# Splitting the F2 and F3 products of a convolution into odd and even nodes, with their differences on GpSimd

## The chip, the cores and the metric

One NeuronCore of a Trainium2 chip. The metric is the device time of one execution in microseconds; the kernel before takes 300.03 us (median of 3 runs, 299.94 to 300.22).

## The reference, cut to what matters

32 graphs of 256 nodes with 128 features each, all in fp32. One layer:

```python
xc = transpose(x)                                        # (32, 128 features, 256 nodes)
h = relu(bn1(conv1d(xc, conv1_w, taps=1)))
h = bn2(conv1d(h, conv2_w, taps=17, pad=8))              # 128 x 128 x 17
x_conv = transpose(relu(h + xc))
s = x @ w_se.T + b_se                                    # 3 per node
dist = |s_n|^2 + |s_m|^2 - 2 s_n.s_m
x_nmp = (exp(-dist) * adj) @ relu(x @ w_msg.T + b_msg)
gru = GRUCell(input=[x_conv, x_nmp], state=x)            # gates r, z, n
out = layernorm(x + gru)
```

The costliest part is the 17-tap convolution, and the change is in it alone.

## The kernel before, in words

The graphs go in 4 groups of 8. A group is 2048 columns (8 graphs of 256 nodes) in 4 chunks of 512 on 128 partitions. Each fp32 operand that TensorE reads is split in a high and a low part of type fp32r (ScalarE copies the high part, VectorE subtracts for the low one), and a product is three matrix instructions (`three`, L358): high by high, high weight by low operand, low weight by high operand.

The convolution works on nodes in 4 phases (node number modulo 4), so that the 17 taps fall into phases too, and saves products by differences of phases: `PRODUCTS` (L57) has nine, called n = 0 to 8: H3, D2, D3, E1, F0, E3, F1, F2, F3. Each is 4 taps of 3 instructions over 512 columns (5 taps where an extra tap belongs to it). H3, E1 and E3 are shared by two outputs and are made in `shared_bank`; the F products go to `side_bank[0]` and `side_bank[1]` in turn, on top of a copy of the shared bank. F rows are differences of E rows, which are differences of the hidden rows H; VectorE makes them in `EF` chunk by chunk (`late_differences_e`, `late_differences_f`, L1201 and L1207), two chunks in the gate stage and two in the mix stage. `late_hi` (L770) and `late_lo` (L1219) split them into `V_hi`, `V_lo` (F0 to F3) and `T_hi`, `T_lo` (E1 and E3).

In groups 1 to 3, E1 and E3 are split once more, into odd and even nodes: `third` (L445) makes two taps' worth of products over the odd nodes alone (256 columns, with sums of tap pairs, `tw_hi`, `tw_lo`) in a distance bank, `pre` (L787) on ScalarE spreads them over both halves of the shared bank, and `halves` (L456) adds products of 256 columns over differences of neighbouring nodes. Group 0 makes all nine in full.

A group alternates between two stages on all engines. In the mix stage (`mix_stage`, L535 on TensorE, L816 on ScalarE, L1358 on VectorE) TensorE makes the nine products with the distances and gathers (the graph sums, `gather`, L429) between them. In the gate stage (`gru_stage`, L656, L909, L1474) it makes the gates chunk by chunk, with conv1 and the messages of the next group. The order on every engine is written out by hand, and semaphores tie the engines: `x_ready` counts low parts of x, which `conv1(g + 1, k)` needs in gate stage k; `m_ready` counts low parts of the graph sums, which the gather two graphs later needs; `copy_ready` counts copies of the shared bank; `vb_ready` the late low parts. GpSimd makes only the powers of the layer norm (`chunk_rstd`, L1044) and a scaled identity (L1050). The queue of SP issues the loads in a fixed order, each behind waits.

## Time and profile before

| | |
|---|---|
| median of 3 runs | 300.03 us |
| profiled execution | 300.24 us, span 298.4 us |
| instructions in the span | 4842 |
| TensorE busy | 290.2 us, 97%, 1455 products |
| VectorE busy | 230.0 us, 77% |
| ScalarE busy | 199.0 us, 67% |
| GpSimd busy | 23.8 us, 8% |
| granted TensorE clock, share of full | 0.997 |

The span is the time from the first to the last instruction on the core; the execution's own time has 1.8 us more around it. Busy shares are averages over all stages. A matrix instruction's listed duration (0.40 us for 512 columns) overlaps the next one's, so what one costs in a row is read from start to start. The same holds, by some 0.1 us, for VectorE and ScalarE.

### The profile page before, as it was taken

The page shows a single profiled execution, that of the slowest core. Times are in us where ns is not written, and L with a number is a line of the kernel's source. Part 1 is how long each engine was busy: PE and PEld are TensorE (multiplying, and loading weights), DVE is VectorE, ACT ScalarE, POOL GpSimd, SP SyncE. Part 2 cuts the span into 40 slices and gives each one's busy share as a digit, 9 for nine tenths or more (in the row PEclk, how much of TensorE's full clock was granted, in tenths as well). Part 3 has the DMA queues.
Part 4 walks back from the last instruction along what each step waited for, and adds up shares of the span by engine and source line. Part 5 has one row for each costly group of instructions (what it writes and reads, how often), then busy time and mean ns, then how long its engine had stood idle before and what let it go on. Part 6 is the DMA issues. An engine that isn't in the chain of part 4 may idle for free.

```text
span 298.4 us, 4842 instructions
## 1 busy us (share of the span) xinstructions
PE 290.2 (97%) x1455; PEld 237.9 (80%) x1455; DVE 230.0 (77%) x647; ACT 199.0 (67%) x442; POOL 23.8 (8%) x49
## 2 busy tenths in 40 slices
PE   8999999999999999999999999999999999999991
PEld 6787787888887988888887888888888898888871
DVE  2799899499969966459979976459978996525793
ACT  2879756488867678378775769368884759624354
POOL 3100000000000240000000070000000042000122
PEclk9999999999999999999999999999999999999998
DMA  7502436422003323701203222712211041510002
GB/s 249 219 0 74 142 141 191 163 70 70 24 32 92 127 84 87 268 10 62 70 35 105 70 70 104 252 65 70 70 35 35 0 141 70 141 69 0 30 7 105
DMA packets 12256, 27.23 MB, mean 91 GB/s; under 512 B 1362, under 2 KB 2132, under 8 KB 12116
## 3 DMA queue, kind: packets, MB, share of 16 engines
q1 hardware_dynamic: 11956, 26.03, 26.1%
q10 hardware_dynamic: 288, 1.05, 1.0%
q8 instruction: 6, 0.10, 0.1%
q14 instruction: 6, 0.05, 0.1%
HBM read 22.88 MB, written 4.19 MB: 91 GB/s over the span
## 4 chain that ended last, share of the span: by engine, by line
PE 92%; DVE 4%; issue 1%; POOL 1%; ACT 1%; POOLq 0%; DVEq 0%
PE bank L356 89%; PE bank L614 2%; PE bank L409 1%; DVE first L1296 1%; POOL rstd L1014 1%; DVE xr L1503 0%; DVE xr L1508 0%; ACT hn L933 0%; POOLq L84 0%; DVE first L1302 0%; DVE xn L1309 0%; DVE hn L1496 0%; DVE hn L1325 0%; ACT z L930 0%; DVE hn L1328 0%
## 5 line engine op out<-in xcount | busy, mean ns | idle before, releaser
L356 PE MATMUL bank<-x_hi,w_hl 128*128 128x512 f32 x120 | 44.2, 409 | 0.0
L356 PE MATMUL bank<-ec_hi,w_hl 128*128 128x512 f32 x96 | 35.4, 396 | 0.0
L356 PE MATMUL bank<-m_hi,w_hl 128*128 128x512 f32 x96 | 35.2, 399 | 0.0
L356 PE MATMUL bank<-V_hi,cw_hi 128*128 128x512 f32 x68 | 28.6, 421 | 0.3 <-ACT bank L785 0.3
L356 PE MATMUL bank<-V_lo,cw_hi 128*128 128x512 f32 x68 | 27.2, 400 | 0.0
L356 PE MATMUL bank<-V_hi,cw_lo 128*128 128x512 f32 x68 | 27.1, 398 | 0.0
L356 PEld LDWEIGHTS bank<-x_hi,w_hl 128*128 128x128 f32 x120 | 22.6, 188 | 5.3 <-DVE x_lo L1154 0.5
L1488 DVE SCALAR_TENSOR_TENSOR hn<-xr,hn 128x512 f32<-128x512 f32 x15 | 10.4, 690 | 18.4 <-ACT hn L921 18.4
L1012 POOL TENSOR_TENSOR rstd<-first,pconst 128x4 f32<-128x4 f32 x15 | 3.5, 233 | 260.8 <-DVE first L1302 260.8
L785 ACT ACTIVATE bank<-bank 128x512 f32<-128x512 f32 x24 | 13.6, 582 | 15.1 <-PE bank L356 10.7
L356 PE MATMUL bank<-x_lo,w_hl 128*128 128x512 f32 x60 | 23.7, 394 | 0.0
L812 ACT ACTIVATE xn<-xn,shift,rstd 128x128 f32<-128x128 f32 x48 | 19.1, 480 | 6.0 <-DVE shift L1316 6.0
L356 PE MATMUL bank<-ec_hi,cw_hi 128*128 128x512 f32 x56 | 23.1, 412 | 0.0
L920 ACT ACTIVATE xr<-bank,vec 128x512 f32<-128x512 f32 x16 | 11.0, 690 | 17.8 <-PE bank L356 17.8
L356 PE MATMUL bank<-ec_lo,cw_hi 128*128 128x512 f32 x56 | 22.4, 400 | 0.0
L356 PE MATMUL bank<-ec_hi,cw_lo 128*128 128x512 f32 x56 | 22.3, 399 | 0.0
L356 PEld LDWEIGHTS bank<-ec_hi,w_hl 128*128 128x128 f32 x96 | 18.1, 188 | 4.5
L356 PEld LDWEIGHTS bank<-m_hi,w_hl 128*128 128x128 f32 x96 | 18.0, 188 | 4.3
L356 PE MATMUL bank<-m_lo,w_hl 128*128 128x512 f32 x48 | 19.1, 397 | 0.0
L356 PE MATMUL bank<-ec_lo,w_hl 128*128 128x512 f32 x48 | 19.0, 395 | 0.0
L356 PE MATMUL bank<-first,xr 128*128 128x132 f32 x128 | 18.1, 281 | 0.0
L1281 DVE SCALAR_TENSOR_TENSOR ec_lo<-H,ec_hi 128x512 fp32r<-128x512 f32 x16 | 11.0, 686 | 9.0 <-ACT ec_hi L806 8.9
(165 smaller groups left out, 749.8 us busy)
## 6 DMA issues: line engine op xcount, KB each, us to landing
adj<-adj_dram SPq DMA_DIRECT2D x16, 512.0 KB, 4.9
x<-xt_dram SPq DMA_DIRECT2D x16, 256.0 KB, 3.2
xn<-xn_dram SPq DMA_DIRECT2D x16, 256.0 KB, 4.6
out_dram<-xn SPq DMA_DIRECT2D x15, 256.0 KB, 2.1
xr<-xt_dram SPq DMA_DIRECT2D x12, 256.0 KB, 3.6
xn<-wcv_dram SPq DMA_DIRECT2D x1, 1024.0 KB, 7.5
xr<-xt_dram ACTq DMA_DIRECT2D x1, 768.0 KB, 5.8
EF<-wsm_dram SPq DMA_DIRECT2D x1, 512.0 KB, 3.2
```

Of the source, the lines that this page charges most:

```text
L356: return nc.tensor.matmul(out, lhs, rhs, start=start, stop=stop, skip_group_check=True)
L409: last = nc.tensor.transpose(out[:, i * N + mb * P:i * N + (mb + 1) * P], f32(U[:, i, mb]).rearrange("p b k -> p (b k)"), idn[:, :])
L614: turned = nc.tensor.transpose(turn_bank[k][:, j * P:(j + 1) * P], r[:, k % 2, j * P:(j + 1) * P], idn[:, :])
L785: nc.scalar.activation(side_bank[side][:, :], shared_bank[:, :], ACT.Copy).then_inc(copy_ready, 1)
L812: last = nc.scalar.activation(xn[:, n, :], xn[:, n, :], ACT.Identity, bias=shift[:, k, n - NB * k:n - NB * k + 1], scale=rstd[:, n:n + 1])
L920: nc.scalar.activation(r[:, k % 2, :], r_bank[:, :], ACT.Tanh, bias=v(BR), scale=0.5).then_inc(r_ready, 1)
L1012: nc.gpsimd.tensor_tensor(dst, src, eps.broadcast_to(shape), ALU.add).then_inc(eps_added, 1)
L1014: return nc.gpsimd.tensor_tensor(dst, dst, pconst[:, 2:3].broadcast_to(shape), ALU.pow)
L1281: STT(phase(c_lo, c), inner(c), 0.0, f32(phase(c_hi, c)), ALU.max, ALU.subtract).then_inc(c_ready, 1)
L1296: last = nc.vector.bn_stats(stats[:, NB * k + j, :], node_rows(k)[:, j, :])
L1488: STT(hk, rk, 1.0, hk, ALU.add, ALU.mult).then_inc(gated_ready, 1)
```

## The change

In groups 1 to 3 the products F2 and F3 are made as E1 and E3 already are. Per group the 24 instructions of 512 columns become 12 over odd nodes (`third(g, 2)` and `third(g, 3)`, behind product 5, both in distance bank 0) and 24 of 256 columns (`halves`). The even rows and the "next" differences come from GpSimd (`third_rows`, in place in `EF`, and a new row 10 of it). ScalarE and VectorE split them in `late_hi_f` and `late_lo_f`: chunks 0 and 1 in the gate stage at the end of k = 1 and 2, chunks 2 and 3 in the mix stage. ScalarE keeps the odd results in `hn` (`keep_thirds`); VectorE writes shared bank plus odd results into the side banks (`add_third`), in place of ScalarE's copies `shared(g, 2, 0)` and `shared(g, 2, 1)`. The sums of tap pairs for F2 and F3 are made in group 0 in place in the loaded taps (`setup_pair_taps`, `pair_taps_hi`, `setup_pair_taps_lo`); SP's loads of the node rows, which overwrite the taps, wait for them.

To make room, F2 and F3 leave `V`, and the high and low parts of the first two pairs' graph sums go to slots of `T` whose products are done (`pair_sums`), so their copies also wait for product 3 or 5. The pre-sum `P1` lives in `hn` in all groups (the wait of `half` for `vb_ready` goes), the norm's scale and shift live in `mv`, and the scaled identity lives in the rows of the bias and is made behind GpSimd's loop. On ScalarE `weights(g, 7)` moves ahead of `sums_hi(g, 1)`, on VectorE `mask(g, 6)` ahead of `sums_lo(g, 1)`. `pre` counts `third_done` by four a group.

```diff
-NE, NF4, NT = 3, 4, 2
+NE, NV, NT, NTE = 3, 2, 4, 2
+THIRD = {7: 0, 8: 1, 5: 2, 6: 3}
...
-        EF = sb("EF", [P, 2, 10, QS])
-        V_hi, V_lo = sb("V_hi", [P, NF4, SL], F32R), sb("V_lo", [P, NF4, SL], F32R)
+        EF = sb("EF", [P, 2, 11, QS])
+        V_hi, V_lo = sb("V_hi", [P, NV, SL], F32R), sb("V_lo", [P, NV, SL], F32R)
...
+        def pair_sums(t, k):
+            if k < 2:
+                at = k * (3 * HQ)
+                return (T_hi if t is m_hi else T_lo)[:, k].rearrange("p k m -> p (k m)")[:, at:at + CH]
+            return t[:, (k - 2) * CH:(k - 1) * CH]
...
+        def woven(t):
+            return t.rearrange("p a (m h b) -> p a m h b", h=2, b=2)
+        def next_diff(k):
+            return EF[:, k % 2, 10, :].rearrange("p (a j) -> p a j", a=2)[:, :, 0:HQ - 2]
...
-            sp.wait_ge(cw_ready, NP)
+            sp.wait_ge(tw_ready, 2)
...
+                n = (3, 5, 7, 8)[i]
+                bank = dist_bank[(0, 1, 0, 0)[i]][:, CH // 2 * (i == 3):CH // 2 * (i == 3) + CH // 2]
                 taps = [(tw_hi[:, 2 * i + s], tw_lo[:, 2 * i + s], s) for s in range(2)]
-                if PRODUCTS[SHARED[i + 1]][2]:
+                if PRODUCTS[n][2]:
                     taps.append((cw_hi[:, TAPS - 1], cw_lo[:, TAPS - 1], 2))
                 for wh, wl, s in taps:
-                    vh, vl = (t[:, :, 2 * s:2 * s + RUN // 2] for t in v)
-                    last = three(bank[:, 0:CH // 2], wh, wl, vh, vl, s == 0, False)
+                    if i < NTE:
+                        vh, vl = (t[:, i, :, 2 * s:2 * s + RUN // 2] for t in (T_hi, T_lo))
+                    else:
+                        vh, vl = (woven(t[:, i, :, 0:QS])[:, :, s:s + RUN // 4, 1] for t in (T_hi, T_lo))
+                    last = three(bank, wh, wl, vh, vl, s == 0, False)
                 last.then_inc(third_done, 1)
...
-            def halves(n, extra):
-
-                i = SHARED.index(n) - 1
-                f = PRODUCTS[n][1]
-                out = shared_bank[:, :].rearrange("p (x h b) -> p h x b", h=2, b=2)
+            def halves(n, extra, bank):
+                slot, f = PRODUCTS[n][0:2]
+                i = THIRD[slot]
+                out = bank[:, :].rearrange("p (x h b) -> p h x b", h=2, b=2)
                 for t in range(TG + extra):
-                    w = TAPS - 1 if t == TG else TAPS + TG * (f - 4) + t
-                    at = (1 + t % 2) * HQ + 2 * (t // 2)
-                    vh, vl = (v[:, i, :, at:at + RUN // 2].rearrange("p k (m b) -> p k m b", b=2) for v in (T_hi, T_lo))
+                    w = TAPS - 1 if t == TG else (4 * t + f if f < 4 else TAPS + TG * (f - 4) + t)
+                    m = t // 2
+                    if i >= NTE and t % 2 == 0:
+                        vh, vl = (woven(v[:, i, :, 0:QS])[:, :, m:m + RUN // 4, 0] for v in (T_hi, T_lo))
+                    else:
+                        at = (1 + t % 2) * HQ + 2 * m
+                        vh, vl = (v[:, i, :, at:at + RUN // 2].rearrange("p k (m b) -> p k m b", b=2)
+                                  for v in (T_hi, T_lo))
                     last = three(out[:, t % 2].rearrange("p (k m) b -> p k m b", k=NC), cw_hi[:, w, :], cw_lo[:, w, :],
                                  vh, vl, False, t == TG + extra - 1)
...
+                    elif n == 5:
+                        pe.wait_ge(exp_ready, 8 * g + 5)
+                        pe.wait_ge(vc_ready, 4 * g)
+                        third(g, 2)
+                        third(g, 3)
...
             def sums_hi(g, pair):
                 act.wait_ge(nmp_done, 8 * g + 2 * pair + 2)
-                nc.scalar.activation(chunk(m_hi, pair), nmp_bank[:, :], ACT.Copy).then_inc(mhi_ready, 1)
+                if pair < 2:
+                    act.wait_ge(conv2_done, NP * g + (4, 6)[pair])
+                nc.scalar.activation(pair_sums(m_hi, pair), nmp_bank[:, :], ACT.Copy).then_inc(mhi_ready, 1)
...
+            def keep_thirds(g):
+                act.wait_ge(third_done, 4 * g)
+                act.wait_ge(t_step, 4 * g + 4)
+                nc.scalar.activation(hn[:, 0, :], dist_bank[0][:, :], ACT.Copy).then_inc(thirds_kept, 1)
+            def late_hi_f(g, k):
+                act.wait_ge(third_ready, 4 * g + k - 3)
+                nc.scalar.activation(T_hi[:, NTE:, k, 0:QS], EF[:, k % 2, 6:8, :], ACT.Copy)
+                nc.scalar.activation(T_hi[:, NTE:, k, QS:QS + HQ - 2], next_diff(k), ACT.Copy).then_inc(vchi_ready, 1)
...
-                if side == 0 and not first:
-                    act.wait_ge(vb_ready, 4 * g)
-                P1 = P1_first if first else P1_later
...
+                    pair_taps_hi()
                     gates_hi()
...
+                late_hi_f(g, 2)
                 pre(g, 0)
                 operands(g, 1)
                 half(g, 1, first)
+                late_hi_f(g, 3)
...
+                weights(g, 7)
                 sums_hi(g, 1)
-                weights(g, 7)
+                keep_thirds(g)
                 relu2(g, 0)
-                shared(g, 2, 0)
                 normalise_rows(g - 1, 2)
                 normalise_rows(g - 1, 3)
-                shared(g, 2, 1)
...
+                        if k in (1, 2):
+                            late_hi_f(g + 1, k - 1)
...
+            def third_rows(g, k):
+                pool.wait_ge(f_step, 4 * g + k + 1)
+                rows = woven(EF[:, k % 2, 6:8, :])
+                even, odd = rows[:, :, :, 0], rows[:, :, :, 1]
+                nxt = next_diff(k).rearrange("p a (m b) -> p a m b", b=2)
+                nc.gpsimd.tensor_tensor(nxt, even[:, :, 1:], odd[:, :, 0:HQ // 2 - 1],
+                                        ALU.subtract).then_inc(odd_step, 1)
+                pool.wait_ge(odd_step, 4 * g + k + 1)
+                nc.gpsimd.tensor_tensor(even, even, odd, ALU.subtract).then_inc(third_ready, 1)
+            with pool.Fori(0, NG - 1) as g:
+                for k in range(NC):
+                    third_rows(g, k)
+                for k in range(NC):
+                    chunk_rstd(g, k)
+            pool.wait_ge(bias_set, 8 * (NG - 1))
             pool.wait_ge(idn_loaded, 16)
             nc.gpsimd.tensor_scalar(idn4[:, :], idn[:, :], 4.0, None, ALU.mult).then_inc(idn4_ready, 1)
-
-            with pool.Fori(0, NG - 1) as g:
-                for k in range(NC):
-                    chunk_rstd(g, k)
...
+            def setup_pair_taps():
+                for f in (2, 3):
+                    last = TT(tap_pairs(f)[:, :, 0], tap_pairs(f)[:, :, 0], tap_pairs(f)[:, :, 1], ALU.add)
+                last.then_inc(tsum_ready, 1)
+            def setup_pair_taps_lo():
+                dve.wait_ge(twhi_ready, 2)
+                for f in (2, 3):
+                    at = slice(2 * f, 2 * f + 2)
+                    last = STT(tw_lo[:, at, :], tap_pairs(f)[:, :, 0], -1.0 if f % 2 else 1.0, f32(tw_hi[:, at, :]),
+                               ALU.mult, ALU.subtract)
+                last.then_inc(tw_ready, 1)
...
+            def late_lo_f(g, k):
+                dve.wait_ge(vchi_ready, 4 * g + k - 3)
+                TT(T_lo[:, NTE:, k, 0:QS], EF[:, k % 2, 6:8, :], f32(T_hi[:, NTE:, k, 0:QS]), ALU.subtract)
+                TT(T_lo[:, NTE:, k, QS:QS + HQ - 2], next_diff(k), f32(T_hi[:, NTE:, k, QS:QS + HQ - 2]),
+                   ALU.subtract).then_inc(vc_ready, 1)
+            def add_third(g, side):
+                dve.wait_ge(conv2_done, NP * g + 6)
+                dve.wait_ge(thirds_kept, g)
+                dve.wait_ge(t_ready, 4 * g + side + 1)
+                out, own = (b[:, :].rearrange("p (x h b) -> p x h b", h=2, b=2) for b in (side_bank[side], shared_bank))
+                odd = hn[:, 0, side * (CH // 2):(side + 1) * (CH // 2)].rearrange("p (x o b) -> p x o b", o=1, b=2)
+                TT(out, own, odd.broadcast_to([P, CH // 4, 2, 2]), ALU.add).then_inc(copy_ready, 1)
...
+                    dve.wait_ge(cw_ready, NP)
+                    setup_pair_taps()
                     conv_sum(g, 1, first)
                     mask(g, 6)
                     mask(g, 7)
                     split_x(0, 0, True)
                     conv_lo(g, 1)
                     conv_sum(g, 2, first)
+                    setup_pair_taps_lo()
                     setup_gates_lo()
...
+                late_lo_f(g, 2)
+                late_lo_f(g, 3)
                 mask(g, 4)
                 mask(g, 5)
                 conv_sum(g, 0, first)
+                mask(g, 6)
                 sums_lo(g, 1)
-                mask(g, 6)
+                add_third(g, 0)
                 conv_lo(g, 0)
                 mask(g, 7)
                 conv_sum(g, 1, first)
+                add_third(g, 1)
...
                         d_lo(g + 1, k)
+                        if k in (1, 2):
+                            late_lo_f(g + 1, k - 1)
```

## Rows read from the trace of the kernel before

**Rows 1.** The page, busy time of each engine, share of the span, instructions

```profile
PE 290.2 (97%) x1455; PEld 237.9 (80%) x1455; DVE 230.0 (77%) x647; ACT 199.0 (67%) x442; POOL 23.8 (8%) x49
```

**Rows 2.** The page, the chain that ended last, shares by engine

```profile
PE 92%; DVE 4%; issue 1%; POOL 1%; ACT 1%; POOLq 0%; DVEq 0%
```

**Rows 3.** Timeline of TensorE, second mix stage: start us, us, engine, line, operation, operands

```profile
98.03 0.28 PE L356 MATMUL bank<-T_hi,tw_hi 128*128 128x256 f32 x1
...
99.85 0.60 PE L409 MATMUL bank<-idn,U 128*128 128x128 f32 x4
...
109.86 0.28 PE L356 MATMUL bank<-T_lo,cw_hi 128*128 128x256 f32 x1
...
111.20 0.40 PE L356 MATMUL bank<-V_hi,cw_hi 128*128 128x512 f32 x1
...
118.62 0.40 PE L356 MATMUL bank<-V_hi,cw_hi 128*128 128x512 f32 x1
...
121.46 1.03 PE L356 MATMUL bank<-z,msg 128*128 128x256 f32 x4
```

**Rows 4.** Weight loads by line: busy us, mean ns (packed, then strided)

```profile
L356 PEld LDWEIGHTS bank<-x_hi,w_hl 128*128 128x128 f32 x120 | 22.6, 188 | 5.3 <-DVE x_lo L1154 0.5
...
L356 PEld LDWEIGHTS bank<-first,xr 128*128 128x128 f32 x128 | 16.9, 196 | 0.5 <-issue 0.2
```

**Rows 5.** Timeline of VectorE, then TensorE, group 0

```profile
45.30 0.74 DVE L1276 SCALAR_TENSOR_TENSOR H<-bank,vec,H 128x512 f32<-128x512 f32 x1
...
50.76 0.68 DVE L1263 TENSOR_TENSOR m_lo<-bank,m_hi 128x512 fp32r<-128x512 f32 x1
...
51.58 1.10 PE L356 MATMUL bank<-z,msg 128*128 128x256 f32 x4
```

**Rows 6.** Timeline of VectorE in the first gate stage that prepares a next group

```profile
67.39 0.72 DVE L1222 TENSOR_TENSOR V_lo<-EF,V_hi 128x544 fp32r<-128x544 f32 x1 [0.32 <-ACT T_hi L774]
68.03 0.29 DVE L1224 TENSOR_TENSOR T_lo<-EF,T_hi 128x136 fp32r<-128x136 f32 x1
68.24 0.43 DVE L1225 TENSOR_TENSOR T_lo<-EF,T_hi 128x272 fp32r<-128x272 f32 x1
68.59 0.68 DVE L1496 TENSOR_TENSOR hn<-hn,bank 128x512 f32<-128x512 f32 x1
...
81.12 0.69 DVE L1154 TENSOR_TENSOR x_lo<-xr,x_hi 128x512 fp32r<-128x512 f32 x1 [0.20 <-ACT x_hi L707]
```

**Rows 7.** Timeline of ScalarE in the same gate stage

```profile
66.71 0.32 ACT L773 ACTIVATE T_hi<-EF 128x136 fp32r<-128x136 f32 x1
66.93 0.43 ACT L774 ACTIVATE T_hi<-EF 128x272 fp32r<-128x272 f32 x1
67.25 0.78 ACT L713 ACTIVATE H<-bank,vec 128x512 f32<-128x512 f32 x1
...
80.46 0.63 ACT L707 ACTIVATE x_hi<-xr 128x512 fp32r<-128x512 f32 x1
```

**Rows 8.** Timeline of weight loads (PEld) in the same gate stage

```profile
66.12 0.19 PEld L356 LDWEIGHTS bank<-x_hi,w_hl 128*128 128x128 f32 x1 [0.19 <-DVE x_lo L1154]
...
81.58 0.19 PEld L356 LDWEIGHTS bank<-ec_hi,w_hl 128*128 128x128 f32 x1
81.87 0.19 PEld L356 LDWEIGHTS bank<-x_hi,w_hl 128*128 128x128 f32 x1
```

**Rows 9.** Timeline of GpSimd; then VectorE's line 1109: duration ns min/median/max

```profile
9.76 0.82 POOL L1050 TENSOR_SCALAR idn<-idn 128x128 f32<-128x128 f32 x1 [2.36 <-DMA idn<-idn_dram]
...
L1109 DVE TENSOR_TENSOR x<-xn x4: 685/690/775, 9.5 to 16.7; 128x512 f32<-128x512 f32 x4
```

**Rows 10.** Timelines of VectorE and ScalarE, second mix stage

```profile
108.70 0.16 DVE L1316 SCALAR_TENSOR_TENSOR shift<-first,rstd 128x4 f32<-128x4 f32 x1 [1.09 <-POOL rstd L1014]
...
109.75 0.58 ACT L748 ACTIVATE z<-bank 128x512 f32<-128x512 f32 x1
```

More of the change, by code:

```diff
@@ L119, in build @@
         msg = sb("msg", [P, GB, MB, P])
-        m_hi, m_lo = sb("m_hi", [P, C], F32R), sb("m_lo", [P, C], F32R)
+        m_hi, m_lo = sb("m_hi", [P, 2 * CH], F32R), sb("m_lo", [P, 2 * CH], F32R)
         ec_hi, ec_lo = sb("ec_hi", [P, C + CH], F32R), sb("ec_lo", [P, C + CH], F32R)
@@ L235, in whole, with tap_pairs @@
             return t[:, s - F0, :].rearrange("p (k m) -> p k m", k=NC)[:, :, 0:width]
+        def pair_sums(t, k):
[3 more added lines that the diff above has]
+            return t[:, (k - 2) * CH:(k - 1) * CH]
+        def tap_pairs(f):
+            return taps[:, 0:TAPS - 1, :].rearrange("p (s two k) o -> p s two k o", two=2, k=4)[:, :, :, f]
+        def woven(t):
+            return t.rearrange("p a (m h b) -> p a m h b", h=2, b=2)
+        def next_diff(k):
+            return EF[:, k % 2, 10, :].rearrange("p (a j) -> p a j", a=2)[:, :, 0:HQ - 2]
         def phase(t, c):
@@ L488, in conv2 @@
                     pe.wait_ge(pre_ready, 2 * g - 2 + SHARED.index(n))
-                    halves(n, extra)
+                    halves(n, extra, shared_bank)
+                    return
+                if n >= 7 and not first:
+                    halves(n, extra, side_bank[n - 7])
                     return
@@ L498, in conv2 @@
                     w = 4 * t if t == TG else (4 * t + f if f < 4 else TAPS + TG * (f - 4) + t)
-                    if slot >= E1:
-                        vh, vl = (v[:, slot - E1, :, 2 * t:2 * t + RUN] for v in (T_hi, T_lo))
+                    if slot in THIRD:
+                        vh, vl = (v[:, THIRD[slot], :, 2 * t:2 * t + RUN] for v in (T_hi, T_lo))
                     else:
@@ L560, in mix_stage @@
                         gather(g, n - 1, first)
+                    elif n == 5:
[3 more added lines that the diff above has]
+                        third(g, 3)
             def gates(g, k, last):
-                xk, mk, ck = ((chunk(a, k), chunk(b, k)) for a, b in ((x_hi, x_lo), (m_hi, m_lo), (c_hi, c_lo)))
+                xk, mk, ck = ((f(a, k), f(b, k)) for f, a, b in ((chunk, x_hi, x_lo), (pair_sums, m_hi, m_lo), (chunk, c_hi, c_lo)))
                 def part(out, w, v, start=False, stop=False):
@@ L619, in gates_final @@
                 k = NC - 1
-                xk, mk, ck = ((chunk(a, k), chunk(b, k)) for a, b in ((x_hi, x_lo), (m_hi, m_lo), (c_hi, c_lo)))
+                xk, mk, ck = ((f(a, k), f(b, k)) for f, a, b in ((chunk, x_hi, x_lo), (pair_sums, m_hi, m_lo), (chunk, c_hi, c_lo)))
                 def part(out, w, v, start=False, stop=False):
@@ L766, in slot_high @@
                 act.wait_ge(done, n)
-                dst = T_hi[:, slot - E1, :, 0:QS] if slot >= E1 else whole(V_hi, slot, QS)
+                dst = T_hi[:, THIRD[slot], :, 0:QS] if slot in THIRD else whole(V_hi, slot, QS)
                 nc.scalar.activation(dst, src.rearrange("p (k m) -> p k m", k=NC), ACT.Copy).then_inc(slot_hi, 1)
@@ L963, in tap_hi, with pair_taps_hi @@
                 nc.scalar.activation(dst, src, ACT.Copy, scale=-1.0 if f % 2 else 1.0).then_inc(cwhi_ready, 1)
+            def pair_taps_hi():
+                act.wait_ge(tsum_ready, 2)
+                for i in (2, 3):
+                    last = nc.scalar.activation(tw_hi[:, 2 * i:2 * i + 2, :], tap_pairs(i)[:, :, 0], ACT.Copy,
+                                                scale=-1.0 if i % 2 else 1.0)
+                last.then_inc(twhi_ready, 1)
             def gates_hi():
@@ L1196, in slot_low @@
                 dve.wait_ge(slot_hi, n)
-                dst, hi = ((t[:, slot - E1, :, 0:QS] for t in (T_lo, T_hi)) if slot >= E1
+                dst, hi = ((t[:, THIRD[slot], :, 0:QS] for t in (T_lo, T_hi)) if slot in THIRD
                            else (whole(t, slot, QS) for t in (V_lo, V_hi)))
@@ L1262, in sums_lo @@
                 dve.wait_ge(mhi_ready, 4 * g + pair + 1)
-                TT(chunk(m_lo, pair), nmp_bank[:, :], f32(chunk(m_hi, pair)),
+                TT(pair_sums(m_lo, pair), nmp_bank[:, :], f32(pair_sums(m_hi, pair)),
                    ALU.subtract).then_inc(m_ready, 1)
@@ L1268, in base @@
                 dve.wait_ge(p_ready, 2 * g + c % 2 + 1)
-                P1 = P1_first if first else P1_later
                 TT(inner(c), grid(P1[:, c % 2, :]), phase(x[:, :], c), ALU.add).then_inc(t_step, 1)
@@ L1350, in final_chunk @@
                 norm_shift(g, k - 1)
-                norm_shift(g, k)
+                norm_shift(g, k, 3)
                 for j in range(3):
```

39 lines of the change are left out of this document (20 added, 19 removed).

## The prediction, made before the changed kernel ran

> **What bounds the kernel now.** I read the engine totals first, then the chain of waits, then the matrix engine's timeline, and last the timelines of VectorE and ScalarE at the few places where the matrix engine is released just in time. TensorE is busy 97% of the span [rows 1] and 92% of the chain that ended last is TensorE [rows 2]. So each product that it no longer does counts in full, and a new wait costs only where its slack is already nil. VectorE is at 77% and ScalarE at 67% on average, but both have stretches with no idle time at all, and there an added instruction moves all that follows it.
>
> **What TensorE loses and gains.** For groups 1 to 3 the products of F2 and F3 were 24 instructions of 512 columns. Twelve of these take 118.62 to 121.46, 0.2367 us each [rows 3], so 5.68 us go. They come back as 24 instructions of 256 columns (halves) and 12 of 256 (thirds, two taps of three products each, twice). The existing thirds run fifteen in 98.03 to 99.85, 0.1213 us each, and the existing halves eleven in 109.86 to 111.20, 0.1218 each [rows 3]. 36 x 0.1215 = 4.38 us. The net is 1.30 us a group, 3.90 us over three. Group 0 keeps its full products.
>
> What no row shows: 24 of the 36 read their moving operand in pairs of nodes with a gap of two (`woven`), where the existing halves read packed rows. Nearest rows: weight loads that take every second element last 196 ns against 188 for packed ones [rows 4], so almost nothing; at the other end such a read walks over as much memory as a 512-column one and could last 0.237 instead of 0.1215, 24 x 0.115 = 2.8 us a group. Faster than packed it can't be, since columns are as many. I take the first: it is a row of the same array's own reads. The Trainium skill (SBUF — State Buffer, Specifications) says that reads go at full rate with two hits in each 16-byte line; four-byte pairs in every second slot give just two, so by that rule too nothing is lost. No row here shows it for a moving operand.
>
> **Set-up, group 0.** VectorE works without idle time here, from 45.30 to 50.76 and beyond [rows 5]. The change puts four operations of 256 elements into this stretch: two pair sums ahead of the convolution sum at 45.30, two low parts ahead of the gate weights. One of 272 takes 0.35 from start to start, 68.24 to 68.59 [rows 6], so one of 256 0.34, and 4 x 0.34 plus a wait for its own last result of about 0.1 is 1.45 us. The row at 50.76 makes the low part of pair 2's sums, ends at 51.44, and TensorE starts the gather that waits for it at 51.58 [rows 5], right behind the last product. There is no slack, so the full 1.45 us is a stall, once. ScalarE's two copies of the pair taps (0.32 each by the 272-element row, [rows 7]) end before VectorE asks for them. Bounds 0.9 (half absorbed) to 1.9. The loads of the node rows and of group 1's first x on SP now wait for this too, some 5 us later; the first x low part then ends at about 60.2 where TensorE asks at 60.4 with the stall in, so I add nothing, up to 0.5 in the range.
>
> **ScalarE in the gate stage.** In group iterations k=1 and k=2 it gets a copy of the F rows (272 elements, 0.32 from start to start) and of the next differences (132, 0.22) behind the second message [rows 7]; the V copy shrinks by 0.21. At k=1 the idle time before the next x high part takes it. At k=2 there is none: x high part 3 started at 80.46 [rows 7], right behind the message. It now starts 0.54 later, and with it the low part on VectorE, which waited for it at 81.12 [rows 6]. The weight load that needs this low part was itself held by it and began at 81.87, 0.29 behind the one at 81.58 [rows 8], where undisturbed ones keep the 0.237 of their products [rows 3]; its matrix product was not late yet, so it had about 0.08 left. So 0.54 + 0.03 - 0.08 = 0.49 us of stall in each of three groups. The 0.03 is VectorE's own account ahead of that: low parts of V cost 0.35 instead of 0.64 [rows 6], twice, plus a wait that shortens, and two new low-part operations cost 0.35 + 0.21.
>
> **GpSimd against VectorE.** GpSimd now runs two operations of 132 and 136 elements per chunk, from the moment the F differences are there, that is beside VectorE's low part of x at 65.4. That result also has no slack: its load sat 0.19 us for it [rows 8]. The one GpSimd operation of this size took 0.82 us [rows 9]; while it ran, one of four equal VectorE operations took 775 ns instead of 685 to 690 [rows 9], so 0.09 per operation, 0.18 per chunk. Two chunks lie in the gate stage: the first delays x low part 1 (0.18), the second runs on into x low part 3, where the 0.18 already lost counts in TensorE's favour. Sum per group 0.49 + 0.18 = 0.67, over three 2.0 us. Bounds of this share: 0, and 1.64 per chunk if VectorE is held for all of it. GpSimd's own length doesn't matter (0.2 to 1.7 each): its results are read 6 us later.
> The Trainium skill (SBUF — State Buffer, Terms) says the two engines' shared port pair is locked for a whole instruction and the loser fully blocks. The trace speaks against the full price: by it the operation above should have been held for most of the 0.82.
>
> **The rest of the mix stage** is hidden. ScalarE's and VectorE's late F parts (0.54 and 0.56 a chunk) fall into idle time: the shift at 108.70 is followed by 1.5 us of waiting for the exponential that starts at 109.75 [rows 10], so both are done by 110.0; the thirds start at 111.20. Then, all on the new clock of TensorE: thirds to 112.66, F1 to 115.5, gathers to 117.05, F2 to 118.7, F3 to 120.16. The copy of the thirds ends at 113.45 (a 512-column copy, 0.58 as in the exponential row [rows 10]); the first sum on VectorE ends at 114.2, wanted at 117.05; the second needs F1 and its convolution sum and ends at 117.25, wanted at 118.7. Both sums I price as 0.7; at twice that they still fit. The low part of pair 2's sums ends at about 119.05, wanted at 120.16. ScalarE stands waiting for the thirds until 112.85; queued behind it are the first relu, whose low part VectorE makes next, and eight norm rows, which end at 117.1 on this clock; then the second relu, whose sum is ready at 116.5, so 0.6 us late at worst and with 9 us to its reader. The second and third wait added, for product 3 or 5 ahead of the graph sums' high parts, is over before ScalarE comes to them or 0.3 us behind. If this cover goes, the first to be late is that last one, 1.1 us away. One ScalarE copy of the shared bank less per group, and a moved GpSimd product for the identity (0.82, forty us before its use), cost nothing.
>
> **Sum.** -3.90 + 1.45 + 2.00 = -0.45 us. The profiled execution took 300.24 (span 298.4 and 1.8 around it), so 299.8 for its like; against the median of 300.03 it is 299.6. What this measurement can tell from no change is 0.2%, 0.6 us.
>
> **Rivals.**
> (a) The stalls are not there, in whole or in part: the releases turn out to have slack, since ScalarE gets to its copies sooner or TensorE's queue runs ahead. For it: ScalarE idles a third of the time. Against: both releases show up as waits in the rows. All gone: 300.03 - 3.90 = 296.1; only the set-up stall left 297.6, only the gate-stage ones left 298.1.
> (b) The slower side: GpSimd holds VectorE for its whole operation. At the place named, chunk 0 beside x low part 1, 2 x 0.82 = 1.64 us of stall per group and 0.49 as before: 3 x 2.13 = 6.4, so -3.90 + 1.45 + 6.4 = +3.95, 304.0. It decides from 0.33 us per chunk on, where the sum is zero. For it: a zero slack at 66.12 [rows 8] and VectorE full from there to 81. Against: the 0.09 of rows 9. By the rule of the skill cited above this would be the outcome.
> (c) The gapped reads cost like 512 columns: +8.3 on the forecast, 307.9. Half of that for a partly slowed read. Against: the loads of [rows 4].
> (d) The new adds or thirds come late for products 7 or 8 and a new wait opens in the mix stage: beyond 1.1 us of slack, each 0.3 is 0.9 over three groups.
>
> **How the numbers follow.** The forecast's mechanism has 0.50, with a range of its own of 299.1 (GpSimd costs nothing) to 300.6; (a) 0.20; (b), whole or half, 0.16; (c) 0.08; (d) 0.06. Faster by over 0.6 us is all of (a) and a third of the forecast: 0.38. Within 0.6: most of the rest of it and weak forms of (b) and (d): 0.36. Slower: 0.26. The range from 297.4 leaves out the cleanest (a), up to 303.0 leaves out full (b) and (c).
>
> **What would show it.** TensorE: thirds F at 0.122 each and the whole group 1.3 us shorter between its first product and its first gate; if they read 0.15 or more, (c). Waits: the weight load of x_hi in the fourth chunk waiting for VectorE's x_lo by about 0.5 us, three times; the gather in group 0 waiting for VectorE's m_lo by about 1.45, once. VectorE: x_lo or the short differences beside GpSimd lasting 0.09 longer; if 0.4 and more, (b). I am wrong in kind if the waits of TensorE stay as they are and time falls by more than 2.4 us, or if a wait for the shared or side banks shows up ahead of F2 or F3.

## The result, and the profile after

The changed kernel takes 310.0 us (309.39 to 310.2, four runs) against 300.12 (299.94 to 300.58, four runs) of the kernel before, measured with it: a ratio of 1.0309 with a 95% interval of 1.0285 to 1.0333. It is 9.9 us slower where 299.6 was forecast, and lies outside the range of 297.4 to 303.0. The profiled execution took 309.39, with a span of 307.0, so 9.15 more than its like before, 8.6 of them inside the span.

The page of the changed kernel, engine totals (as in [rows 1]) and the chain that ended last, by engine (as in [rows 2]):

```profile
PE 295.2 (96%) x1491; PEld 243.6 (79%) x1491; DVE 244.5 (80%) x681; ACT 201.4 (66%) x465; POOL 40.2 (13%) x73
...
PE 73%; DVE 15%; DMA 4%; issue 3%; ACT 2%; POOL 1%; SPq 1%; POOLq 0%; DVEq 0%; ACTq 0%
```

TensorE is 5.0 us busier, though it streams fewer columns, and VectorE has gone from 4% of the chain to 15%: products got dearer and new waits opened. To separate the two I compare how long one group takes on TensorE, from one second mix stage to the next. The matrix products on `idn,U` that follow the thirds are a good mark: before, they start at 99.85 [rows 3] and at 169.67, a period of 69.82 us. The timeline of TensorE in the changed kernel (start us, us, engine, line, operation, operands) has the same mark, then the thirds and halves of F2 and F3:

```profile
100.44 0.28 PE L375 MATMUL bank<-T_hi,tw_hi 128*128 128x256 f32 x1
...
102.27 0.49 PE L428 MATMUL bank<-idn,U 128*128 128x128 f32 x3
...
113.63 0.39 PE L375 MATMUL bank<-T_hi,tw_hi 128*128 128x256 f32 x1
...
116.36 0.41 PE L375 MATMUL bank<-V_hi,cw_hi 128*128 128x512 f32 x1
...
120.76 0.57 PE L375 MATMUL bank<-T_hi,cw_hi 128*128 128x256 f32 x1
...
123.04 0.39 PE L375 MATMUL bank<-T_hi,cw_hi 128*128 128x256 f32 x1
...
125.18 0.38 PE L375 MATMUL bank<-z,msg 128*128 128x256 f32 x1
...
174.54 0.60 PE L428 MATMUL bank<-idn,U 128*128 128x128 f32 x4
```

The period is now 174.54 - 102.27 = 72.27, so 2.45 us more a group. The reader sees two kinds of product of 256 columns. The old fifteen thirds, with packed rows, still run in 100.44 to 102.27, 0.122 each. The twelve new thirds, with gapped rows, take 113.63 to 116.36, 0.2275 each, nearly as long as products of 512 columns (0.2367 [rows 3]). The halves of F2 and F3, half of them gapped, take 2.28 (with a slow first one) and 2.14 us for twelve each, where packed ones would take 1.46. Over 24 gapped products that is 24 x 0.1075 = 2.58 us a group. A group then stands at -1.30 (the saved columns) + 2.58 = +1.28, and the other 1.17 of its 2.45 I put down to waits; the two stalls read below, 0.16 and 0.95, make 1.11 of it. Times three, plus 1.30 for group 0 (below): 3 x 2.45 + 1.30 = 8.65, beside the 8.6 by which the span grew.

The waits, as the list of waits of the changed kernel has them (us in total, times, longest):

```profile
PEld bank L375 <- DVE x_lo L1239: 5.0, 6, 1.2
...
PE bank L375 <- DVE x_lo L1239: 2.3, 3, 0.8
...
ACT x_hi L743 <- DMA xr<-xt_dram: 2.0, 1, 2.0
```

TensorE waits for x low part 1 and 3 in each of three gate stages, and in group 0 for the low part of pair 2's sums. In the same timeline of TensorE, group 0:

```profile
51.24 0.40 PE L375 MATMUL bank<-T_hi,cw_lo 128*128 128x512 f32 x1
52.82 0.45 PE L375 MATMUL bank<-z,msg 128*128 128x256 f32 x1 [1.17 <-DVE m_lo L1363]
```

The gather comes 1.58 us after the last product instead of some 0.28, so the set-up costs 1.30 (1.45 predicted). Now x low part 1, in the timeline of the four engines (the changed kernel):

```profile
66.21 0.53 POOL L1113 TENSOR_TENSOR EF<-EF 128x132 f32<-128x132 f32 x1 [58.78 <-DVE EF L1297]
...
66.38 0.51 DVE L1302 TENSOR_TENSOR EF<-EF 128x132 f32<-128x132 f32 x1
66.82 0.95 POOL L1116 TENSOR_TENSOR EF<-EF 128x136 f32<-128x136 f32 x1
66.82 0.68 DVE L1239 TENSOR_TENSOR x_lo<-xr,x_hi 128x512 fp32r<-128x512 f32 x1
...
67.42 0.65 DVE L1259 TENSOR_TENSOR ec_lo<-EF,ec_hi 128x272 fp32r<-128x272 f32 x1
67.55 0.19 PEld L375 LDWEIGHTS bank<-x_hi,w_hl 128*128 128x128 f32 x1 [0.45 <-DVE x_lo L1239]
```

While GpSimd works, VectorE's operation of 132 elements takes 0.51 us and its 272-element one 0.65; an equal one of 272 without GpSimd beside it takes 0.43 [rows 6]. x_lo itself, at 0.68, is not lengthened. So about 0.22 for each of GpSimd's operations, 0.45 a chunk, where I had 0.18. One of the two stands ahead of x low part 1, so x_lo starts 0.22 later; TensorE's product that needs it comes 0.40 behind the one before instead of 0.24, 0.16 late.

The ends of these operations show how the two engines share. GpSimd's first one ends at 66.74, VectorE's beside it at 66.89; x_lo ends at 67.50, GpSimd's second one at 67.77, VectorE's next at 68.07. So it goes for all 24 of GpSimd's difference operations: each ends 0.27 us behind a VectorE operation, and the next VectorE operation ends 0.15 (132 or 136 elements) or 0.30 (272) behind it. The two take turns: GpSimd waits for x_lo, which is why it takes 0.95, and VectorE's operation behind waits for GpSimd. GpSimd's listed time holds its own wait, and only some 0.22 of it is a delay for VectorE.

And x low part 3, same kernel and view, ScalarE then VectorE then the weight load:

```profile
82.42 0.43 ACT L823 ACTIVATE T_hi<-EF 128x272 fp32r<-128x272 f32 x1
...
82.74 0.31 ACT L824 ACTIVATE T_hi<-EF 128x132 fp32r<-128x132 f32 x1
...
82.94 0.62 ACT L743 ACTIVATE x_hi<-xr 128x512 fp32r<-128x512 f32 x1
...
83.60 0.69 DVE L1239 TENSOR_TENSOR x_lo<-xr,x_hi 128x512 fp32r<-128x512 f32 x1 [0.65 <-ACT x_hi L743]
...
84.35 0.19 PEld L375 LDWEIGHTS bank<-x_hi,w_hl 128*128 128x128 f32 x1 [1.23 <-DVE x_lo L1239]
```

The two new copies on ScalarE stand straight ahead of x high part 3 (0.52 us from 82.42 to 82.94), VectorE idles 0.65 until that part is there, and TensorE's product, 1.19 behind the one before instead of 0.24, is 0.95 late.

Outside the span stand 2.39 us instead of 1.84. Other versions below show between 1.8 and 2.4 with no order that I can name; this half microsecond stays open.

### The profile page after: what moved, and what is told of

Same layout as the page of the kernel before. It is cut to its first block, busy times and chain, and to the rows that moved or that the text cites. A ratio compares the mean times of both kernels' runs of the same rounds, so it can differ in the third digit from the quotient of the medians.

```text
span 307.0 us, 5006 instructions
## 1 busy us (share of the span) xinstructions
PE 295.2 (96%) x1491; PEld 243.6 (79%) x1491; DVE 244.5 (80%) x681; ACT 201.4 (66%) x465; POOL 40.2 (13%) x73
## 4 chain that ended last, share of the span: by engine, by line
PE 73%; DVE 15%; DMA 4%; issue 3%; ACT 2%; POOL 1%; SPq 1%; POOLq 0%; DVEq 0%; ACTq 0%
PE bank L375 71%; DMA z<-wcv_dram 2%; PE bank L650 2%; DMA x<-xt_dram 1%; DVE H L1369 1%; DVE x L1180 1%; DVE first L1395 1%; DVE cw_lo L1196 1%; DVE x_lo L1239 1%; POOL first L1072 1%; DVE xr L1358 1%; DVE T_lo L1284 1%; DVE EF L1278 1%; ACT x_hi L743 1%; DVE xr L1609 0%
## 5 line engine op out<-in xcount | busy, mean ns | idle before, releaser
L1113 POOL TENSOR_TENSOR EF<-EF 128x132 f32<-128x132 f32 x12 | 6.4, 530 | 191.3 <-DVE EF L1297 191.3
L375 PE MATMUL bank<-T_hi,cw_hi 128*128 128x256 f32 (+1 forms) x71 | 25.6, 360 | 0.0
L375 PE MATMUL bank<-T_hi,cw_lo 128*128 128x256 f32 (+1 forms) x71 | 23.7, 334 | 0.0
L375 PE MATMUL bank<-T_lo,cw_hi 128*128 128x256 f32 (+1 forms) x71 | 23.7, 333 | 0.0
L859 ACT ACTIVATE xn<-xn,first 128x128 f32<-128x128 f32 x48 | 19.1, 485 | 6.9 <-DVE first L1415 6.9
L835 ACT ACTIVATE bank<-bank 128x512 f32<-128x512 f32 x18 | 10.1, 583 | 14.2 <-PE bank L375 9.0
L375 PE MATMUL bank<-m_hi,w_hl 128*128 128x512 f32 x48 | 18.1, 401 | 0.0
L375 PE MATMUL bank<-z,msg 128*128 128x256 f32 x64 | 16.9, 386 | 1.2 <-DVE m_lo L1363 1.2
L375 PEld LDWEIGHTS bank<-first,xr 128*128 128x128 f32 x128 | 16.9, 196 | 0.5 <-issue 0.2
L375 PE MATMUL bank<-T_hi,w_hl 128*128 128x512 f32 x48 | 17.0, 396 | 0.0
```

Of the source, the lines that this page charges most:

```text
L375: return nc.tensor.matmul(out, lhs, rhs, start=start, stop=stop, skip_group_check=True)
L835: nc.scalar.activation(side_bank[side][:, :], shared_bank[:, :], ACT.Copy).then_inc(copy_ready, 1)
L859: last = nc.scalar.activation(xn[:, n, :], xn[:, n, :], ACT.Identity, bias=shift[:, k, n - NB * k:n - NB * k + 1], scale=rstd[:, n:n + 1])
L1113: nc.gpsimd.tensor_tensor(nxt, even[:, :, 1:], odd[:, :, 0:HQ // 2 - 1], ALU.subtract).then_inc(odd_step, 1)
```

## Experiments

Three things have to be told apart: the gapped reads (7.7 us), the contention of GpSimd with VectorE, and the place of the late copies. An undo of one term should return just that term.

**packed.** The changed kernel, with the F rows laid down packed.

```diff
-    vh, vl = (woven(t[:, i, :, 0:QS])[:, :, s:s + RUN // 4, 1] for t in (T_hi, T_lo))
+    vh, vl = (t[:, i, :, HQ + 2 * s:HQ + 2 * s + RUN // 2] for t in (T_hi, T_lo))
...
-    nc.scalar.activation(T_hi[:, NTE:, k, 0:QS], EF[:, k % 2, 6:8, :], ACT.Copy)
+    for h in range(2):
+        nc.scalar.activation(packed(T_hi, k, h), f_rows(k, h), ACT.Copy)
```

(and so the halves, and VectorE's low parts)

> The changed kernel with the F rows of T laid out as the E rows are: even differences in the first 68 columns of a chunk, odd nodes in the next 68, so that TensorE reads packed rows in all 36 instructions; ScalarE and VectorE write them with two operations of 136 elements instead of one of 272. Theory A (the gapped reads cost 0.23 us instead of 0.12): 24 instructions a group fall by 0.107 each, 2.6 us a group, 7.7 over three; the extra operation costs ScalarE 0.12 in front of x high part 3 in each group, 0.4 in all. 302.7 us. Rival (the reads cost nothing and the loss is in waits on VectorE, GpSimd or the set-up): 310 as the changed kernel, or a little more.

Measured: 302.54 us against 300.51 of the kernel before, ratio 1.0055 (1.0039 to 1.0071). Against the changed kernel that is 7.5 us less, for the same products with the same columns and a few more operations on ScalarE and VectorE. The group period falls from 72.27 to 69.89. The gapped reads are thereby shown as the main cause; what is left over the kernel before is stalls: 69.89 - (69.82 - 1.30) = 1.37 a group and 1.4 in group 0. In this profiled execution there is one more. The later load of group 1's x holds ScalarE's x high part for 3.7 us, and TensorE's first product on that x comes 0.89 behind the one before, 0.65 late, where the changed kernel still had slack.

**nopool.** The changed kernel; GpSimd's differences are left out (the even rows and row 10 then hold no differences; a memset fills row 10 once, ahead of the loop).

```diff
-                for k in range(NC):
-                    third_rows(g, k)
...
-                act.wait_ge(third_ready, 4 * g + k - 3)
+                act.wait_ge(ef_ready, 4 * g + k - 3)
```

> The changed kernel without GpSimd's two difference operations per chunk (the even rows and the next differences are left out; what reads them goes on when VectorE's F differences are done). Theory: two VectorE operations per chunk last 0.22 longer beside GpSimd (0.51 instead of 0.29, 0.65 instead of 0.43), 0.45 per chunk; the first chunk's 0.22 stands before x low part 1, the second's 0.45 before x low part 3, together about 0.67 a group, so 308.0. Rival (GpSimd is paid in idle time of VectorE): 310. Rival (the skill's full lock is the main loss): below 306.

Measured: 307.44, ratio 1.0234 (1.019 to 1.0278), 2.6 us under the changed kernel. The period falls from 72.27 to 71.65, so 0.62 a group; the span of the profiled execution falls by 1.7 (307.0 to 305.3), and the rest of the 2.6 I can't place. Its VectorE timeline shows the two operations at their own length again:

```profile
66.54 0.30 DVE L1301 TENSOR_TENSOR EF<-EF 128x132 f32<-128x132 f32 x1
...
67.35 0.44 DVE L1258 TENSOR_TENSOR ec_lo<-EF,ec_hi 128x272 fp32r<-128x272 f32 x1
```

So the difference of 0.21 on each is GpSimd's doing. The stalls left in its trace, 71.65 of period + 1.30 - 2.58 - 69.82 = 0.55 a group, are what the late copies cost by themselves; read at the product that waits for x low part 3, 0.73 behind the one before instead of 0.24, they are 0.49.

**move.** The changed kernel, chunk 1's late F copies and low parts at the end of k=3.

```diff
-                        if k in (1, 2):
-                            late_hi_f(g + 1, k - 1)
+                        if k in (1, 3):
+                            late_hi_f(g + 1, k // 2)
```

(and so `late_lo_f` on VectorE)

> The changed kernel with chunk 1's late F parts (ScalarE's and VectorE's) at the end of k = 3 of the gate stage instead of k = 2, so that nothing new stands ahead of x high part 3. Theory: the stall of TensorE for x low part 3 (0.8 us a group by the matrix row's idle time, some 0.95 with the part that weight loads hide) goes, 0.22 stays at x low part 1: 307.2. Rival (VectorE's chain, slowed by GpSimd and by the low parts of chunk 0, is late by itself): half of it or less, 308.6 and above.

Measured: 309.57, ratio 1.0291 (1.0257 to 1.0325): a miss, 0.4 us under the changed kernel where 307.2 was expected, with a period of 72.18 against 72.27. ScalarE's copies no longer stand ahead of x high part 3 and the stall there falls from 0.95 to 0.42, but VectorE's own chain is late there by GpSimd's 0.45, and the work put off to the end now meets the thirds of E. The timeline of TensorE shows this new wait:

```profile
172.04 0.40 PE L375 MATMUL bank<-ec_hi,cw_lo 128*128 128x512 f32 x1
172.61 0.35 PE L375 MATMUL bank<-T_hi,tw_hi 128*128 128x256 f32 x1 [0.17 <-DVE T_lo L1310]
```

That product is 0.33 late (0.57 behind the one before instead of 0.24). Each cause alone keeps about half of the stall at x low part 3, 0.42 here and 0.49 in nopool, and what this order gives back there it loses almost whole again, most of it at the thirds.

**strides.** What exactly of a gapped read costs? The kernel before, with the thirds of E reading other columns (their sums are then over other nodes): five patterns, each a run of so many words and a gap of so many.

```diff
-                    vh, vl = (t[:, :, 2 * s:2 * s + RUN // 2] for t in v)
+                    run, gap = ((2, 2), (1, 1), (4, 4), (8, 8), (2, 2))[3 * i + s]
+                    n = RUN // 2 // run
```

> The kernel before, where the thirds over E1 and E3 read their moving operand in other patterns (so the sums are over other columns): five taps of three instructions with 256 columns in 4 chunks, in the order pairs with a gap of 2, single elements with a gap of 1, runs of 4 with a gap of 4, runs of 8 with a gap of 8, pairs again. Theory S1 (time goes by the addresses walked over): all fifteen 0.23 us from start to start. Theory S2 (time goes by the number of breaks, 0.83 ns each by the pairs' 0.228 against 0.1215): single elements 0.335, pairs 0.228, runs of four 0.175, runs of eight 0.148. Theory S3 (the skill's rule of two hits in each 16-byte line): pairs and single elements with a gap of 1 both 0.12; the changed kernel speaks against it. In time: S1 4.8 us more than before (15 x 0.107 x 3), S2 about 4.

Measured: 303.46 in one run (before 300.51). Its timeline of TensorE; each of the five patterns is three products, so the steps between these rows are three products each (the last row ends the fifth):

```profile
98.36 0.39 PE L356 MATMUL bank<-T_hi,tw_hi 128*128 128x256 f32 x1
...
99.03 0.41 PE L356 MATMUL bank<-T_hi,tw_hi 128*128 128x256 f32 x1
...
99.72 0.30 PE L356 MATMUL bank<-T_hi,cw_hi 128*128 128x256 f32 x1
...
100.09 0.28 PE L356 MATMUL bank<-T_hi,tw_hi 128*128 128x256 f32 x1
...
100.45 0.40 PE L356 MATMUL bank<-T_hi,tw_hi 128*128 128x256 f32 x1
...
101.13 0.40 PE L409 MATMUL bank<-idn,U 128*128 128x128 f32 x2
```

Pairs 0.223, single words 0.230, runs of four 0.123, runs of eight 0.120, pairs 0.227. Gap and distance are not it: runs of eight with a gap of eight walk over just as much memory as pairs with a gap of two, and are free. Nor is it the number of breaks, for pairs and singles cost the same. The Trainium skill (SBUF — State Buffer, Specifications), which I had weighed in the prediction, asks for at least two accesses in each 16-byte line for full bandwidth, and I had read that as enough. Its same row adds that each crossing into a new line pays a penalty, which I had not weighed; lines and words below try a price per line. The trace speaks against my reading for this operand: pairs make two accesses in a line and take 0.223 to 0.227, not 0.12.

**lines.** Whether it is the run's length or its place in 16-byte lines (four words).

```diff
+                    run, gap, off, n = ((4, 4, 2, 16), (8, 8, 2, 8), (2, 2, 3, 32), (1, 3, 0, 32), (2, 2, 1, 32))[3 * i + s]
```

> The kernel before, where the thirds over E1 and E3 read other columns again; five taps of three instructions: runs of 4 with a gap of 4 starting 2 words into a 16-byte line; runs of 8 with a gap of 8, starting 2 words in; pairs with a gap of 2 starting at word 3 of a line; single words with a gap of 3 (128 columns only); pairs with a gap of 2 starting at word 1. Theory L (each 16-byte line that an instruction reads costs what 4 columns cost, 1.8 ns, however many words are used): 128 lines 0.228; 96 lines 0.17; 129 lines or 256 visits, 0.23 or 0.45; 128 lines 0.228; 128 lines 0.228. Rival B (only the length of a run counts, and from 4 words on it is free): 0.12, 0.12, 0.228, and for 128 columns of single words 0.115, 0.228.

Measured: 303.71 in one run (before 300.59). TensorE in steps of three products, as above:

```profile
98.22 0.39 PE L356 MATMUL bank<-T_hi,tw_hi 128*128 128x256 f32 x1
...
98.88 0.35 PE L356 MATMUL bank<-T_hi,tw_hi 128*128 128x256 f32 x1
...
99.40 0.40 PE L356 MATMUL bank<-T_hi,cw_hi 128*128 128x256 f32 x1
...
100.07 0.30 PE L356 MATMUL bank<-T_hi,tw_hi 128*128 128x128 f32 x1
...
100.42 0.41 PE L356 MATMUL bank<-T_hi,tw_hi 128*128 128x256 f32 x1
...
101.10 0.41 PE L409 MATMUL bank<-idn,U 128*128 128x128 f32 x2
```

Runs of four that start two words into a line cost 0.220, where the aligned ones cost 0.123: it is the place, not the length. Runs of eight so shifted cost 0.173, in between. Pairs cost 0.223 and 0.227 wherever they start. But 128 single words in 128 different lines took 0.117, half of what a price per line gives. (The runs of 64 of the kernel before show the same effect, small: its thirds that start two words into a line take 98.39 to 98.76 and 99.47 to 99.85, 0.125 each, the other nine 0.119.)

**words.** That last row against a price per word. The kernel before, other patterns again.

```diff
+                    run, gap, off, n = ((2, 6, 0, 24), (1, 3, 0, 48), (48, 2, 0, 1), (32, 2, 0, 1), (6, 2, 0, 10))[3 * i + s]
```

> The kernel before, its five pairs of pair-tap weights of product 3 and 5 reading other columns (their sums are then over other nodes). In order, per 128 partitions and four chunks: pairs with a gap of six (192 columns), single words with a gap of three (192 columns), packed (192), packed (128), runs of six with a gap of two (240). Theory W, a word of a 16-byte line that the run of words leaves partly unread takes 0.89 ns and a word of a fully read line 0.47: 0.171, 0.171, 0.090, 0.060 and (160 x 0.47 + 80 x 0.89) 0.146 us from start to start. Theory L, each partly read line takes 1.8 ns whatever is read of it, and the 0.117 of 128 single words was something else: 0.171, 0.346, 0.090, 0.060, 0.146. Theory M, a product of few columns has a least time of about 0.117 and that is what the 128 single words showed, while a partly read line costs 1.8 ns: the packed 128 columns also show 0.117, and the 192 single words 0.346. Time of the whole: 0.5 to 1 us off the 303.5 that the other kernels of this kind gave, no claim on it.

Measured: 301.25 in one run (before 300.95). TensorE, in the same steps:

```profile
97.90 0.34 PE L356 MATMUL bank<-T_hi,tw_hi 128*128 128x192 f32 x1
...
98.41 0.35 PE L356 MATMUL bank<-T_hi,tw_hi 128*128 128x192 f32 x1
...
98.93 0.27 PE L356 MATMUL bank<-T_hi,cw_hi 128*128 128x192 f32 x1
...
99.27 0.25 PE L356 MATMUL bank<-T_hi,tw_hi 128*128 128x128 f32 x1
99.35 0.28 PE L356 MATMUL bank<-T_lo,tw_hi 128*128 128x128 f32 x1
99.46 0.27 PE L356 MATMUL bank<-T_hi,tw_lo 128*128 128x128 f32 x1
99.57 0.36 PE L356 MATMUL bank<-T_hi,tw_hi 128*128 128x240 f32 x1
...
100.06 0.60 PE L409 MATMUL bank<-idn,U 128*128 128x128 f32 x4
```

192 columns in pairs 0.170 and in single words 0.173: both 0.89 to 0.90 ns a word, though the singles touch twice as many lines. So L is out, and with it a penalty for each crossing into a new line. Theory W holds for the pairs and the singles. Runs of six (two thirds of their words in full lines) took 0.163 where W gives 0.146; the first product behind the other pattern took 0.19 of that, the second and third 0.15 each. The packed short ones missed: 0.113 and 0.100 for 192 and 128 columns instead of 0.090 and 0.060, and from the second one of 128 columns on it is 0.11 as well. So there is a least time per product of about 0.11 us, part of theory M. The 0.117 of the 128 single words lies right at it and can't tell the theories apart; the 192 single words, at 0.173, can.

**setup.** The changed kernel, the pair taps of F2 and F3 made behind the last low part of the sums of group 0, and the loads of group 1's x ahead of the node rows on SP.

```diff
-                    dve.wait_ge(cw_ready, NP)
-                    setup_pair_taps()
                     conv_sum(g, 1, first)
...
                     sums_lo(g, 3)
+                    dve.wait_ge(cw_ready, NP)
+                    setup_pair_taps()
+                    setup_pair_taps_lo()
                     return
```

> The changed kernel with the sums of tap pairs and their high and low parts at the end of group 0's mix stage instead of inside VectorE's full stretch, and with group 1's first two x loads ahead of the node rows on SP. Theory: the gather in group 0 no longer waits (1.30 us: 1.58 instead of 0.28 from the instruction before it to its first), ScalarE no longer waits 2.0 us for x: 308.7 us, 1.3 less than the changed kernel. Rival (the stall is given back by the next wait in the first gate stage): no change.

Measured: 308.45 against 300.59, ratio 1.0261 (1.0244 to 1.0278), 1.5 us under the changed kernel. The gather follows the last product again (TensorE's timeline):

```profile
51.89 0.40 PE L375 MATMUL bank<-T_hi,cw_lo 128*128 128x512 f32 x1
52.13 1.06 PE L375 MATMUL bank<-z,msg 128*128 128x256 f32 x4
```

**tuned.** Packed rows and the late set-up, GpSimd's work held back until x low part 1 and 3 are made, and the late copies and low parts put where their engines idle.

```diff
                 pool.wait_ge(f_step, 4 * g + k + 1)
+                pool.wait_ge(*((x_ready, 4 * g + 6), (x_ready, 4 * g + 8), (vb_ready, 4 * g + 4), (vb_ready, 4 * g + 4))[k])
...
-                        if k in (1, 2):
-                            late_hi_f(g + 1, k - 1)
+                        if k == 1:
+                            late_hi_f(g + 1, 0)
...
                         h3_hi(g + 1, k)
+                        if k == NC - 1:
+                            late_hi_f(g + 1, 1)
...
-                        if k in (1, 2):
-                            late_lo_f(g + 1, k - 1)
+                        if k == 2:
+                            late_lo_f(g + 1, 0)
...
+                    if not last and k == NC - 1:
+                        late_lo_f(g + 1, 1)
```

> The packed rows of the run before, the late set-up, and another order: GpSimd's chunks 0 and 1 wait for x low parts 1 and 3, its chunks 2 and 3 for VectorE's last low part of V and T; ScalarE's late F copies stand behind the last copy of H in k = 3 (chunk 1) and behind the first graph sums (chunks 2 and 3); VectorE's low parts at the end of k = 2 (chunk 0) and behind the residual of k = 3 (chunk 1). Theory: all that is left is the gain of 36 short for 24 long instructions, 3 x 1.30, and nothing of the set-up: 296.5 to 297.2 against 300.5 of before on this chip, ratio 0.988. Rival (VectorE is simply full, 0.6 us per chunk more work comes out somewhere on the path): 299 to 301.

Measured: 296.48 (296.07 to 297.14) against 300.59, ratio 0.9873 (0.9855 to 0.989). It beats both kernels. Its timelines, TensorE's marks and F thirds, then VectorE with one of GpSimd's operations:

```profile
99.60 0.60 PE L434 MATMUL bank<-idn,U 128*128 128x128 f32 x4
...
110.96 0.28 PE L381 MATMUL bank<-T_hi,tw_hi 128*128 128x256 f32 x1
...
112.44 0.40 PE L381 MATMUL bank<-V_hi,cw_hi 128*128 128x512 f32 x1
...
168.02 0.60 PE L434 MATMUL bank<-idn,U 128*128 128x128 f32 x4
```

```profile
65.18 0.69 DVE L1250 TENSOR_TENSOR x_lo<-xr,x_hi 128x512 fp32r<-128x512 f32 x1
...
65.95 0.54 POOL L1124 TENSOR_TENSOR EF<-EF 128x132 f32<-128x132 f32 x1 [58.52 <-DVE x_lo L1250]
66.14 0.90 DVE L1606 SCALAR_TENSOR_TENSOR hn<-xr,hn 128x512 f32<-128x512 f32 x1
66.96 0.65 DVE L1318 TENSOR_TENSOR V_lo<-EF,V_hi 128x272 fp32r<-128x272 f32 x1
```

The thirds of F cost 0.123 each, and the period is 68.42, 1.40 under that of before. GpSimd still costs VectorE 0.22 twice (0.90 for 0.68, 0.65 for 0.43), but behind x_lo, and TensorE has no wait for x_lo left. VectorE's 0.90 one ends at 67.04, 0.55 behind GpSimd's 66.49: the same turns, with 512 elements.

## Why the prediction was wrong

By its own steps:

- **The gain of TensorE, -1.30 a group.** Right. Tuned, where nothing covers it, shows -1.40; 3.90 in all were forecast for this term, and tuned as a whole is 4.1 under the kernel before (3.3 to 4.4 by the interval of its ratio).
- **The gapped reads, priced at nothing. This is the step that failed.** I chose the 8 ns of a strided weight load [rows 4], "a row of the same array's own reads", over the other end, 24 x 0.115 = 2.8 a group. The measured price is 0.1075 each, 2.58 a group, 7.7 us over three: rival (c), which had 0.08, at nearly its full size of 8.3. Two things made the choice bad. The row at hand was of the stationary operand, and the moving one behaves otherwise. And half of the rule of the Trainium skill (SBUF — State Buffer, Specifications), the two accesses in a line, agreed with it, so that a rule untested here and one row of another operand passed for two witnesses. The sign that I had named for this rival, thirds of F at 0.15 or more, came true. The mean of the two bounds alone would have put the forecast at 303.8.
- **GpSimd beside VectorE, 0.18 a chunk.** Mis-sized: 0.45 a chunk on VectorE, and in nopool all of GpSimd's stalls on TensorE come to 0.62 a group. That is past the 0.33 from which rival (b) decides, and a good third of its 1.64. The row it came from [rows 9] is one overlap, and I read it wrongly. VectorE's first operation on L1109 had started at 9.49, ahead of GpSimd's at 9.76, and took 0.69, so GpSimd's 0.82 was half waiting. The Trainium skill (SBUF — State Buffer, Terms) has the shared port pair locked for a whole instruction and the loser fully blocked. I had taken the trace to speak against the full price; the ends in the changed kernel, 0.27 behind the one and 0.15 or 0.30 behind the other, agree with the turns of that rule. What fails is the listed time as their price: it was 0.53 and 0.95, and VectorE lost 0.22 to each.
- **ScalarE ahead of x high part 3, 0.49.** Right: nopool has 0.49 left at that product and 0.55 in the period. With GpSimd's share the stalls of a group come to 1.17 instead of 0.67, which is 1.5 us of the miss over three groups. That x low part 1's delay would be credited at part 3 was wrong: move shows VectorE late there by itself.
- **The set-up, 1.45 once.** Right in place, 1.30 in size; setup removes it. The load that comes later holds ScalarE's x high part for 2.0 us, and as forecast TensorE doesn't wait for that here; in packed, where it held 3.7, TensorE did, 0.65 once, a little over the 0.5 that I had left for it in the range.
- **The rest of the mix stage, hidden.** Right. No wait for a shared or side bank stands ahead of F2 or F3, even with the thirds and halves 2.6 us longer; that lengthening helped this step, and tuned, without it, has no such wait either.

The sum with the measured terms: -3.90 + 7.74 + 1.30 + 3 x 1.17 = +8.65, beside 8.6 of the span. The 1.17 is what the period leaves, so this sum doesn't prove it; the rows of the two stalls show 1.11 of it. The rest of the 9.15, 0.55, lies outside it and is open.

## What to carry to other kernels

Halving the columns of a product pays only if the words it reads fill whole 16-byte lines: when a change makes a moving operand gapped, pack it with the copy that writes it anyway, and price the gapped read as dear as the full one until a row of the same operand says otherwise. Two small operations on an idle engine aren't free where they lie beside a just-in-time result of another: release them behind that result. When a late result has two causes, one may keep the stall alive without the other: remove both before judging either.

## What the runs showed that I had not expected

- TensorE's moving operand of four-byte words, at a granted clock of 1.00 in these stretches, takes 0.47 ns for a word of a fully read 16-byte line, and 0.89 ns for a word of a line that its run leaves partly unread. That gives 0.228 for 256 columns of pairs or single words (0.223 to 0.230 measured), 0.174 for shifted runs of eight (0.173), 0.171 for 192 words (0.170 and 0.173), and for runs of six 0.146 (0.15 for two of three, 0.163 on average). A start two words into a line nearly doubles the cost of runs of four (0.220 against 0.123) and adds 0.006 to runs of 64 (0.125 against 0.119; the rule gives 0.007). It is a fit to these patterns, each of them run in one kernel; what in the reading makes the price stays open. The weight loads of [rows 4] show no such price (188 ns packed, 196 with every second word).
- With 192 and 128 packed columns the products follow each other by about 0.11 us, not in proportion; what sets this least time wasn't tried.
- GpSimd's differences and VectorE's operations of two inputs in SBUF beside them take turns. Each operation of GpSimd (132 or 136 elements) lengthens one operation of VectorE by 0.22, whether that one has 132, 272 or 512 elements, and is itself lengthened by the one ahead of it: the same 136-element operation is listed with 0.56 us behind a VectorE operation of 136 elements (tuned), 0.70 behind one of 272 and 0.95 behind x_lo's 512 (the changed kernel). What an operation of GpSimd costs VectorE can't be read from its listed time.
